# Local attention: values folded with the output weights before the weighing, fixed key blocks, four accumulating banks

## The chip, the cores and the metric

The kernel runs on one core of one Trainium2 chip. The metric is the device time of one execution in microseconds (us). The profile is one execution taken by the hardware profiler. PE is TensorE's matmuls, PEld its weight loads, DVE is VectorE, ACT ScalarE, POOL GpSimd, SP the queue that issues DMAs. Line numbers such as L1101 are those of the kernel before.

## What is computed

x is 2 x 1024 tokens of 128 features, all in fp32. A grouped latent attention and a stack of six layers both work on the normalised x, and both are added to it. The heads are 16 of 64, the window is 32, DEPTH is 6. Shortened:

```python
x = L0_attn_x
xn = _layernorm(x, axis=-1)
x = x + latent_attention(xn) + local_stack(xn)
# local_stack, for each layer i:
x = attn_layer(shift_tokens(x), Wqkv[i], q_scale[i], k_scale[i], Wo[i]) + x
x = ffn_layer(shift_tokens(x), ln_g[i], ln_b[i], W1[i], b1[i], W2[i], b2[i]) + x
# shift_tokens: the second half of the features comes from the token before
# attn_layer:
qkv = x @ Wqkv;  q, k, v = jnp.split(qkv, 3, -1)
q = l2norm(q) * qs;  k = l2norm(k) * ksc
q = q * cos * scale + rotate_half(q) * sin * scale
k = k * cos * inv + rotate_half(k) * sin * inv
out = local_attention(q, k, v)      # a block of 32 sees itself and the block before
return out @ Wo
# ffn_layer: xn is the layer norm of x, scaled by g and shifted by bln
hg = xn @ W1 + b1
a, gate = jnp.split(hg, 2, -1)
return a * jax.nn.gelu(gate, approximate=False) @ W2 + b2
```

## The kernel before, in words

The program has a latent stage, up to about 380 us, which the change leaves as it is but for where x lies, and then the local stage: 6 layers x 16 tiles of 128 tokens = 96 tiles. The local stage is a software pipeline. A loop over steps G is written out, and in each step every engine executes a fixed list of functions, each for a tile G minus some lag. The feed-forward part works on chunks of four tiles (`chunk_at(G, lag)`), so its functions run in every fourth step. Engines meet only by semaphores, and each engine works its list strictly in order.

TensorE, per tile: keys and queries are projected (`project`: two halves of 512 columns, three fp32r matmuls each, banks 0 and 1). VectorE multiplies them with rotary tables (`cosine` L934, `sine` L939), ScalarE squares, VectorE sums (L961, L966) and makes the first guess of a reciprocal root (`seeds`, L992 to L1000), ScalarE refines it by logarithm and exponential (L764, L766), and GpSimd multiplies it together and scales (L501, L507, L513). Transposes (`transposes`, L1258, eight 128x128 per call, banks 2 and 3) put keys, queries and probabilities in place. `mask_scores` (L1299) and `scores` (L1310, 64 matmuls of 64x32 with 64 columns) fill banks 4 and 5; VectorE takes maxima (L1005) and subtracts (L1011), ScalarE takes the exponential.

The value path is what the change touches. The weighted sum is taken over the shifted input rows themselves: `input_rows` (L1324) transposes them, ScalarE copies them out (L710), and ten DMAs on SP's queue lay them out by window (`xw`). `weigh` multiplies them with the probabilities in two halves of four 64x128 matmuls of 256 columns; ScalarE copies each half (`copy_lower` L717, `copy_upper` L723). `fold` multiplies the result with the products M of value and output weights of each pair of heads, 16 matmuls of 128x128 in two halves. Those products are made once per layer (`products`). `attended` (L981) adds the sum to x. The residual x lies with features on partitions (`X`, `X1`); `ln_rows` (L1399) transposes it for the layer norm, `normalise_rows` (L1020) applies it, `ln_columns` (L1407) transposes back, `down` is three matmuls per chunk with 512 columns, and `residual` (L1063) adds.

Most matmuls are written by one helper, `mm` at L1101; the tile names and shapes tell them apart. Every fp32 matmul leaves two records in the trace, an fp32r one and a transpose leave one.

## Time and profile before

| | us |
|---|---|
| three runs, median (lowest to highest) | 2047.29 (2044.84 to 2058.95) |
| the profiled execution | 2045.28 |
| its span, first to last instruction | 2043.4 |
| TensorE busy | 1873.4 (92%) |
| VectorE busy | 1656.8 (81%) |
| GpSimd busy | 1331.1 (65%) |
| ScalarE busy | 1264.6 (62%) |

Busy time of TensorE is the union of its records, and a record's duration includes latency; back-to-back records overlap. The distance between two starts is the better price of a piece of work. A wait behind an engine that is not the bound costs nothing.

### The profile page before, as it was taken

The numbers are of one execution on the slowest core, as the hardware profiler recorded it, in microseconds if no ns is written. First come the engines' busy times: TensorE is split into PE (matmuls) and PEld (weight loads), VectorE is DVE, ScalarE is ACT, GpSimd is POOL, SyncE is SP. The second block draws the span as 40 slices with busy tenths as digits, with TensorE's granted clock in tenths as the row PEclk, the third lists the DMA queues.
The fourth block names the chain that finished last, engine by engine and source line by source line (L and its number), as shares of the span: only waits on it lengthen the run. The fifth ranks groups of instructions, "written<-read, shape, count | busy, mean of one in ns | idle before, by whom it ended". The sixth has DMA issues, their size and how long they took to land.

```text
span 2043.4 us, 61163 instructions
## 1 busy us (share of the span) xinstructions
PE 1873.4 (92%) x24364; PEld 1471.0 (72%) x24364; DVE 1656.8 (81%) x2684; ACT 1264.6 (62%) x2082; POOL 1331.1 (65%) x1146
## 2 busy tenths in 40 slices
PE   6888887598999999999999999999999999999996
PEld 4655656477777777777777777777777777777774
DVE  4866866577888898898879998898989889887873
ACT  5766665355666566656655666566666666665653
POOL 3322334477778776787767886777777778776760
PEclk9999998799999999999999999999999999999999
DMA  3000000011001110010111101100111001000001
GB/s 106 2 0 0 0 1 6 22 38 38 22 18 24 39 40 17 22 25 18 39 38 22 24 19 39 37 22 22 25 39 38 20 21 24 18 18 15 19 18 27
DMA packets 76933, 50.06 MB, mean 24 GB/s; under 512 B 17216, under 2 KB 74240, under 8 KB 75008
## 3 DMA queue, kind: packets, MB, share of 16 engines
q1 hardware_dynamic: 76672, 46.39, 9.0%
q8 instruction: 187, 3.06, 0.6%
q14 instruction: 74, 0.61, 0.1%
HBM read 20.11 MB, written 1.05 MB: 10 GB/s over the span
## 4 chain that ended last, share of the span: by engine, by line
PE 62%; DVE 23%; issue 9%; ACT 4%; POOL 1%; DMA 1%; DVEq 0%; SPq 0%; ACTq 0%; POOLq 0%
PE banks L1101 44%; PE banks L1258 9%; DVE arena L939 4%; PE banks L1310 4%; DVE arena L934 3%; DVE small L885 2%; PE banks L1185 2%; DVE small L1005 2%; DVE small L966 2%; PE banks L1299 1%; DVE lnx L1020 1%; DVE small L961 1%; DVE arena L1048 1%; DVE small L997 1%; DVE small L972 1%
## 5 line engine op out<-in xcount | busy, mean ns | idle before, releaser
L1101 PE MATMUL banks<-arena 128*128 128x128 f32 (+3 forms) x4516 | 450.9, 280 | 32.3 <-DMA arena<-in_wqT_dram 10.1
L1101 PEld LDWEIGHTS banks<-arena 128*128 128x128 f32 (+3 forms) x4516 | 426.5, 173 | 69.8 <-issue 19.1
L471 POOL TENSOR_TENSOR arena<-arena 128x1024 f32<-128x1024 f32 x96 | 228.8, 2383 | 110.0 <-DVE arena L939 110.0
L934 DVE TENSOR_TENSOR arena<-banks,tabs 128x1024 f32<-128x1024 f32 x192 | 234.3, 1220 | 62.4 <-PE banks L1258 52.7
L703 ACT ACTIVATE arena<-banks 128x1024 f32<-128x1024 f32 x96 | 98.6, 1027 | 230.9 <-PE banks L1258 230.9
L939 DVE TENSOR_TENSOR arena<-banks,tabs 128x1024 f32<-128x1024 f32 x192 | 232.9, 1213 | 0.2 <-issue 0.2
L466 POOL TENSOR_TENSOR prob<-prob,small 128x1024 f32<-128x1024 f32 x96 | 182.8, 1904 | 74.2 <-DVE small L974 70.3
L476 POOL TENSOR_TENSOR arena<-arena 128x1024 f32<-128x1024 f32 x96 | 228.5, 2380 | 0.0
L1101 PE MATMUL banks<-arena,xwr 64*128 64x256 f32 x1536 | 217.8, 402 | 11.3 <-ACT arena L717 11.3
L1101 PE MATMUL banks<-qkH,xsH 128*128 128x512 f32 x384 | 173.7, 452 | 39.6 <-DVE arena L939 39.6
L1258 PE MATMUL banks<-cst,arena 128*128 128x128 f32 x1536 | 209.5, 280 | 0.1
L513 POOL TENSOR_TENSOR arena<-arena,small 128x1024 f32<-128x1024 f32 x96 | 185.1, 1928 | 14.0 <-POOL arena L476 0.4
L1258 PEld LDWEIGHTS banks<-cst,arena 128*128 128x128 f32 x1536 | 176.7, 143 | 21.0 <-issue 1.7
L1101 PEld LDWEIGHTS banks<-arena,xwr 64*128 64x128 f32 x1536 | 132.2, 186 | 81.7 <-issue 47.8
L501 POOL TENSOR_TENSOR small<-small 128x33 f32<-128x33 f32 x100 | 24.7, 247 | 248.3 <-ACT small L766 248.3
L507 POOL TENSOR_TENSOR arena<-arena,small 128x1024 f32<-128x1024 f32 x96 | 182.8, 1904 | 4.4
L966 DVE TENSOR_REDUCE small<-arena 128x16 f32<-128x1024 f32 x96 | 116.8, 1216 | 83.3 <-ACT arena L679 82.9
L394 POOL TENSOR_TENSOR gqs<-arena,cst 128x128 fp32r<-128x128 f32 x112 | 46.0, 411 | 186.9 <-PE banks L1101 157.2
L668 ACT ACTIVATE arena<-banks 128x1024 f32<-128x1024 f32 x96 | 98.5, 1026 | 95.5 <-PE banks L1101 95.5
L1101 PE MATMUL banks<-qkH,xsL 128*128 128x512 f32 x384 | 155.1, 404 | 0.0
L1101 PE MATMUL banks<-qkL,xsH 128*128 128x512 f32 x384 | 154.2, 402 | 0.0
L1310 PE MATMUL banks<-arena 64*32 64x64 f32 x12288 | 143.8, 226 | 10.4 <-issue 9.1
(135 smaller groups left out, 4217.6 us busy)
## 6 DMA issues: line engine op xcount, KB each, us to landing
xwr<-xwr SPq DMA_DIRECT2D x576, 32.0 KB, 1.9
qkraw<-in_wqk_dram SPq DMA_DIRECT2D x6, 1024.0 KB, 5.2
arena<-in_wvo_dram SPq DMA_DIRECT2D x6, 1024.0 KB, 5.2
xwr<-xwr SPq DMA_DIRECT2D x384, 16.0 KB, 1.8
W<-in_w_dram SPq DMA_DIRECT2D x6, 341.0 KB, 3.1
W<-in_w_dram SPq DMA_DIRECT2D x6, 192.0 KB, 2.7
res<-in_x_dram SPq DMA_DIRECT2D x4, 256.0 KB, 4.2
tabc<-in_tab_dram SPq DMA_DIRECT2D x1, 1024.0 KB, 7.5
```

What stands on the lines that cost most here:

```text
L466: pool.tensor_tensor(p, p, over(den[:, :], 64), ALU.mult).then_inc(s["p_nrm"], 1)
L471: pool.tensor_tensor(kc, kc, ks, ALU.add).then_inc(s["k_add"], 1)
L476: pool.tensor_tensor(qc, qc, qs, ALU.add).then_inc(s["q_add"], 1)
L507: pool.tensor_tensor(heads(kc), heads(kc), over(rs[:, 4, 0:LH], LD), ALU.mult).then_inc(s["k_nrm"], 1)
L513: pool.tensor_tensor(heads(qc), heads(qc), over(rs[:, 4, LH:2 * LH], LD), ALU.mult).then_inc(s["q_nrm"], 1)
L703: act.activation(ptile[:, :, :], two(2).rearrange("p (k t) -> p k t", k=NP), ACT.Copy).then_inc(s["pt_cp"], 1)
L934: dve.tensor_tensor(heads(c), heads(two(0)), table(k % NT, kind), ALU.mult).then_inc(s[done], 1)
L939: dve.tensor_tensor(w.rearrange("p (h z k) -> p h z k", h=LH, z=2), swapped(two(0)), table2(k % NT, kind + 1), ALU.mult).then_inc(s[done], 1)
L966: dve.reduce_sum(rin[:, LH:2 * LH], heads(sqq), AXX).then_inc(s["q_ss"], 1)
L1101: return pe.matmul(o, l, r, start=start, stop=stop)
L1258: ins = pe.transpose(bk(2 + k // 4)[:, P * (k % 4):P * (k % 4 + 1)], src[:, P * k:P * (k + 1)], ident)
L1310: ins = pe.matmul(bk(4 + o)[WIN * w:WIN * (w + 1), 64 * j:64 * (j + 1)], qT[r, j, WIN * w:WIN * (w + 1)], kT[r, j, WIN * w:WIN * w + 64], ...
```

## The change

The products of value and output weights are made per layer as before, but split into two fp32r parts (`MH` by ScalarE, `ML` by VectorE's `folded_lower`), and each tile's shifted input is multiplied with them at once (`values`, even and odd heads, banks 4 and 5). ScalarE copies the results, 64 rows at a time, into a ring of six half tiles, `vw`, with 64 keys of the even head on partitions 0 to 63 and of the odd one on 64 to 127. `weigh` then takes probabilities as the stationary operand and `vw` as the moving one, and accumulates over all heads into four banks; VectorE adds the four into the residual. Key blocks of 32 no longer slide: a key block stays on the partitions where it is (`keys_of`, new masks), so a window of odd number is one matmul over 128 rows, and one of even number is four over 32 rows each. The input rows' transposes, copies and DMAs go. The residual (`Xt`) has tokens on partitions: `down` is turned round into 12 matmuls of 128 columns with its bias in a row of ones, `ln_rows` is one matmul with a shift matrix and one for the first row, and `layer_columns` transposes x once per chunk for the next layer. The seeds move from VectorE to GpSimd, with `rin` double. `normalise_rows` is a scalar_tensor_tensor in place of a tensor_scalar. The order of the functions is new on all engines, with larger lags, and STEPS grows from 96 + 11 to 96 + 12. The core of the diff:

```diff
+PV_BANKS, V_BANK, XT_BANK, DN_BANK, LN_BANK = (6, 7, 2, 3), 4, 7, 7, 7
...
+        def keys_of(w):
+            return (slice(0, 5, 4), slice(0, 2, 1), slice(2, 0, -1), slice(2, 4, 1))[w]
...
-                sp.wait_ge(s["xT_cp"], k + 1)
-                if k > 1:
-                    sp.wait_ge(s["z_mm"], 2 * k - 2)
-                now, was = xr[:, k % 2, :], xr[:, (k + 1) % 2, :]
-                for o in range(2):
-                    c0 = 64 * o
-                    sp.dma_start(xw[c0:c0 + WIN, k % 2, 0, :], was[96:P, :]).then_inc(xd_in, 16)
-                    sp.dma_start(xw[c0 + WIN:c0 + 64, k % 2, 0, :], now[0:WIN, :]).then_inc(xd_in, 16)
-                    for w in range(1, NW):
-                        sp.dma_start(xw[c0:c0 + 64, k % 2, w, :], now[WIN * (w - 1):WIN * (w + 1), :]).then_inc(xd_in, 16)
                 if n == 2 and l + 1 < DEPTH:
                     sp.wait_ge(s["wk_L"], l + 1)
                     sp.wait_ge(s["wq_L"], l + 1)
                     load_qk(l + 1)
-                if n == 5 and l + 1 < DEPTH:
+                if n == 3 and l + 1 < DEPTH:
                     sp.wait_ge(s["M_mm"], 2 * l + 2)
                     load_wvo(l + 1)
+                if n == 13 and l + 1 < DEPTH:
+                    sp.wait_ge(s["w1_L"], l + 1)
+                    sp.wait_ge(s["b1_mm"], l + 1)
+                    load_w1(l + 1)
...
+            def seeds(k):
+                if is_tile(k) or is_tile(k - 4):
+                    if is_tile(k):
+                        pool.wait_ge(s["k_ss"], k + 1)
+                        pool.wait_ge(s["q_ss"], k + 1)
+                    after(pool, "ln_eps", k - 3)
+                    after(pool, "rk", k)
+                    pool.tensor_scalar(rs[:, 0, :], rin[:, k % 2, :], 1e-24, None, ALU.max).then_inc(s["r_cl"], 1)
+                    pool.wait_ge(s["r_cl"], k + 1)
+                    pool.tensor_scalar(rs[:, 1, :].bitcast(mybir.dt.int32), rs[:, 0, :].bitcast(mybir.dt.int32), -0.5,
+                                       float(0x5F3759DF), ALU.mult, ALU.add).then_inc(s["r_y0"], 1)
+                    pool.wait_ge(s["r_y0"], k + 1)
+                    pool.tensor_tensor(rs[:, 2, :], rs[:, 1, :], rs[:, 1, :], ALU.mult).then_inc(s["r_q"], 1)
+                    after(pool, "y_ln", k)
+                    pool.wait_ge(s["r_q"], k + 1)
+                    pool.tensor_tensor(rs[:, 3, :], rs[:, 2, :], rs[:, 0, :], ALU.mult).then_inc(s["r_r"], 1)
...
-            def copy_lower(k):
...
-            def copy_upper(k):
...
+            def copy_values(k, o):
+                act.wait_ge(s[f"v_mm{o}"], k + 1)
+                after(act, "o_mm", k - 1)
+                for g in range(2):
+                    act.activation(vw[64 * o:64 * o + 64, (2 * k + g) % RV, :], two(V_BANK)[64 * g:64 * g + 64, :], ACT.Copy)\
+                       .then_inc(s[f"v_cp{o}"], 1)
...
+                    act.activation(lns[:, k % 2, 64:D], bk(LN_BANK)[:, 0:64], ACT.Copy).then_inc(s["ln_cp"], 1)
+                    act.activation(lns[:, k % 2, 0:64], Xt[:, k % TILES, 0:64], ACT.Copy).then_inc(s["ln_cp"], 1)
+            def copy_layer(c):
+                if c is not None and c < (DEPTH - 1) * NC:
+                    act.wait_ge(s["xT_mm"], c + 1)
+                    act.wait_ge(s["xs_L"], 2 * (c + NC))
+                    act.activation(xf[:, :], bk(XT_BANK), ACT.Copy).then_inc(s["xT_cp"], 1)
...
             def attended(k):
                 if is_tile(k):
-                    b, i = tile_at(k)
                     dve.wait_ge(s["o_mm"], k + 1)
-                    after(dve, "x_new", (k - TILES) // 4 + 1)
-                    dve.tensor_tensor(X1[:, b, 1 + P * i:1 + P * (i + 1)], bk(M_BANK)[:, 0:P],
-                                      X[:, b, XO + P * i:XO + P * (i + 1)], ALU.add).then_inc(s["x1"], 1)
-            def seeds(k):
...
+                    x1 = Xt[:, k % TILES, :]
+                    for n, bank in enumerate(PV_BANKS):
+                        after(dve, "x1", NW * k + n)
+                        dve.tensor_tensor(x1, bk(bank)[:, 0:D], x1, ALU.add).then_inc(s["x1"], 1)
...
-                    dve.tensor_scalar(lnx[:, :], lns[:, k % 2, :], ag[:, k % 2, 0:1], rs[:, 4, 32:33], ALU.subtract, ALU.mult)\
-                       .then_inc(s["ln_x"], 1)
+                    dve.scalar_tensor_tensor(lnx[:, :], lns[:, k % 2, :], ag[:, k % 2, 0:1],
+                                             rs[:, 4, 32:33].to_broadcast([P, D]), ALU.subtract, ALU.mult).then_inc(s["ln_x"], 1)
...
+            def folded_lower(l, r):
+                dve.wait_ge(s["M_H"], 2 * l + r + 1)
+                dve.tensor_tensor(halves(ML, r), two(2).rearrange("p (o n) -> p o n", o=2), halves(MH, r), ALU.subtract)                   .then_inc(s["M_L"], 1)
...
+            def values(k, o):
+                b, i = tile_at(k)
+                xH, xL = xsH[:, b, P * i:P * (i + 1)], xsL[:, b, P * i:P * (i + 1)]
+                pe.wait_ge(s["xs_L"], 2 * (k // 4) + 2)
+                pe.wait_ge(s["M_L"], 2 * (k // TILES) + 2)
+                claim(V_BANK, V_BANK + 1)
+                for h in range(2):
+                    c0 = HD * o + 512 * h
+                    mm(bk(V_BANK + h), xH, MH[:, c0:c0 + 512], True, False)
+                    mm(bk(V_BANK + h), xH, ML[:, c0:c0 + 512], False, False)
+                    ins = mm(bk(V_BANK + h), xL, MH[:, c0:c0 + 512], False, True)
+                ins.then_inc(s[f"v_mm{o}"], 1)
...
+            def weigh(k):
                 if is_tile(k):
                     pe.wait_ge(s["pt_cp"], k + 1)
-                    pe.wait_ge(xd_in, XD * (k + 1))
-                    weigh(k, 0)
-            def weigh_upper(k):
-                if is_tile(k):
-                    weigh(k, 1)
-            def fold(r):
-                for q in range(4):
-                    for o in range(2):
-                        ins = mm(bk(M_BANK)[:, 0:P], M[:, r, o, q, :], zT[:, o, :, 4 * r + q, :],
-                                 (r, q, o) == (0, 0, 0), (r, q, o) == (1, 3, 1))
-                return ins
+                    pe.wait_ge(s["v_cp0"], 2 * k + 2)
+                    pe.wait_ge(s["v_cp1"], 2 * k + 2)
+                    pe.wait_ge(s["vw_0"], 1)
+                    claim(*PV_BANKS)
+                    def part(n, w, j, r, at, first, last):
+                        return pe.matmul(bk(PV_BANKS[n])[WIN * w:WIN * (w + 1), 0:D], ptile[r, j, WIN * w:WIN * (w + 1)],
+                                         vw[r, at % RV, D * j:D * (j + 1)], start=first, stop=last, skip_group_check=True)
+                    for j in range(NP):
+                        for w in range(0, NW, 2):
+                            g = 2 * k + w // 2
+                            part(j % NW, w + 1, j, slice(0, P), g, j < NW, j >= NP - NW)
+                            for n in range(NW):
+                                ins = part(n, w, j, slice(WIN * n, WIN * (n + 1)), g - n % 2, j == 0, j == NP - 1)
+                    ins.then_inc(s["o_mm"], 1)
+                    for bank in PV_BANKS:
+                        freed[bank] = ("x1", NW * k + NW)
...
+                    n = k % TILES
+                    pe.wait_ge(s["x1"], NW * k + NW)
+                    claim(LN_BANK)
+                    ins = mm(bk(LN_BANK)[:, 0:64], next_row, Xt[:, n, 64:D])
+                    if n % NT:
+                        ins = pe.matmul(bk(LN_BANK)[0:32, 0:64], first_row, Xt[96:P, n - 1, 64:D], start=False, stop=True,
+                                        skip_group_check=True)
...
-                    for j in range(3):
-                        m = FJ[j][1]
-                        ins = mm(bk(DN_BANK), W2[0:m, c // NC % 2, j, :], gl[j][0:m, :], j == 0, j == 2)
+                    for t in range(4):
+                        for j in range(3):
+                            m = FJ[j][1] + (j == 2)
+                            ins = mm(bk(DN_BANK)[:, P * t:P * (t + 1)], gl[j][0:m, P * t:P * (t + 1)], W2[0:m, c // NC % 2, j, :], j == 0, j == 2)
...
+                transpose_keys(G - 2)
+                values_even(G - 2)
+                weigh(G - 4)
+                project_queries(G - 1)
+                ln_rows(G - 4)
+                transpose_queries(G - 2)
+                values_odd(G - 2)
+                down(chunk_at(G, 12))
+                up_value(chunk_at(G, 11), 0)
+                up_value(chunk_at(G, 10), 1)
+                next_products_lower(G - 2)
+                up_value(chunk_at(G, 10), 2)
+                up_gate(chunk_at(G, 9), 0)
+                up_gate(chunk_at(G, 9), 1)
+                transpose_probs(G - 3)
+                next_shifts(chunk_at(G, 11))
+                mask_scores(G - 2)
+                layer_columns(chunk_at(G, 14))
+                scores(G - 2)
+                up_gate(chunk_at(G, 9), 2)
+                next_products_upper(G - 2)
                 project_keys(G)
-                input_rows(G - 2)
-                transpose_keys(G - 1)
-                weigh_lower(G - 3)
-                up_gate(chunk_at(G, 9), 0)
-                up_value(chunk_at(G, 10), 0)
-                next_products_lower(G - 4)
-                up_gate(chunk_at(G, 9), 1)
-                up_value(chunk_at(G, 11), 2)
-                up_value(chunk_at(G, 10), 1)
-                down(chunk_at(G, 12))
-                weigh_upper(G - 3)
-                next_shifts(chunk_at(G, 12))
-                next_products_upper(G - 4)
-                project_queries(G)
-                transpose_queries(G - 1)
-                up_gate(chunk_at(G, 9), 2)
-                fold_lower(G - 3)
                 ln_columns(G - 5)
-                mask_scores(G - 1)
-                fold_upper(G - 3)
-                scores(G - 1)
-                transpose_probs(G - 2)
-                ln_rows(G - 3)
-                last_rows(chunk_at(G, 13))
```

## Rows read from the trace of the kernel before

**Rows 1.** The page: busy us (share) and instructions, and granted clock in 40 slices

```profile
PE 1873.4 (92%) x24364; PEld 1471.0 (72%) x24364; DVE 1656.8 (81%) x2684; ACT 1264.6 (62%) x2082; POOL 1331.1 (65%) x1146
...
PEclk9999998799999999999999999999999999999999
```

**Rows 2.** The page: chain that ended last, by line

```profile
PE banks L1101 44%; PE banks L1258 9%; DVE arena L939 4%; PE banks L1310 4%; DVE arena L934 3%; DVE small L885 2%; PE banks L1185 2%; DVE small L1005 2%; DVE small L966 2%; PE banks L1299 1%; DVE lnx L1020 1%; DVE small L961 1%; DVE arena L1048 1%; DVE small L997 1%; DVE small L972 1%
```

**Rows 3.** Busy by stage, 500 to 1900 us; columns as its first row

```profile
core 0: us, PE busy (x) PEld busy (x) DVE busy (x) ACT busy (x) POOL busy (x), PEclk, DMA share, GB/s
...
500.00:1900.00 1400.00, 1353.42 (x18863) 1072.23 (x18861) 1227.81 (x1665) 894.83 (x1327) 1046.61 (x773) 1.00 0.11 26
```

**Rows 4.** Waits, 500 to 1900 us: who, for whom, us in total, times, longest

```profile
POOL small L501 <- ACT small L766: 196.3, 83, 4.9
...
PE banks L1101 <- DVE arena L939: 23.6, 34, 0.9
...
PEld banks L1101 <- ACT arena L717: 14.8, 20, 0.8
```

**Rows 5.** TensorE's timeline of a tile: start, us, line, out<-in, tile rows*columns, shape

```profile
812.87 0.28 PE L1324 MATMUL banks<-cst,X 64*128 64x64 f32 x2
813.07 1.09 PE L1258 MATMUL banks<-cst,arena 128*128 128x128 f32 x8
814.10 1.13 PE L1101 MATMUL banks<-arena,xwr 64*128 64x256 f32 x8
815.16 0.47 PE L1101 MATMUL banks<-xnH,W1H 128*85 128x512 f32 x1
...
817.74 0.47 PE L1101 MATMUL banks<-qkH,xsH 128*128 128x512 f32 x1 [0.25 <-DVE arena L939]
...
819.21 1.03 PE L1258 MATMUL banks<-cst,arena 128*128 128x128 f32 x8
820.08 1.95 PE L1101 MATMUL banks<-arena 128*128 128x128 f32 x16
821.87 0.27 PE L1407 MATMUL banks<-cst,lnx 128*128 128x128 f32 x1
...
822.41 1.95 PE L1101 MATMUL banks<-arena 128*128 128x128 f32 x16
824.29 1.48 PE L1310 MATMUL banks<-arena 64*32 64x64 f32 x128
825.70 1.09 PE L1258 MATMUL banks<-cst,prob 128*128 128x128 f32 x8
...
830.82 2.84 PE L1101 MATMUL banks<-arena,W 128*128 128x512 f32 x6
833.59 1.14 PE L1101 MATMUL banks<-arena,xwr 64*128 64x256 f32 x8
```

**Rows 6.** TensorE's timeline in the latent stage

```profile
214.87 1.96 PE L1101 MATMUL banks<-arena 128*32 128x128 f32 x64 [0.55 <-ACT arena L624]
216.75 0.33 PE L1185 MATMUL banks<-cst,arena 128*128 128x128 f32 x1
```

**Rows 7.** VectorE by line and form, 500 to 1900 us: busy, mean ns | idle before

```profile
L1020 DVE TENSOR_SCALAR lnx<-lns,small 128x128 f32<-128x128 f32 x82 | 107.9, 1316 | 0.0
...
L966 DVE TENSOR_REDUCE small<-arena 128x16 f32<-128x1024 f32 x83 | 100.9, 1216 | 71.3 <-ACT arena L679 70.9
...
L1000 DVE TENSOR_TENSOR small<-small 128x33 f32<-128x33 f32 x83 | 47.6, 573 | 8.6
...
L981 DVE TENSOR_TENSOR X<-banks,X 128x128 f32<-128x128 f32 x83 | 23.8, 287 | 16.9 <-PE banks L1101 16.7
...
L992 DVE TENSOR_SCALAR small<-small 128x33 f32<-128x33 f32 x83 | 20.0, 241 | 7.7
```

**Rows 8.** ScalarE by line and form, same window

```profile
L717 ACT ACTIVATE arena<-banks 128x1024 f32<-128x1024 f32 x82 | 84.2, 1027 | 3.7
```

**Rows 9.** GpSimd by line and form, same window

```profile
L501 POOL TENSOR_TENSOR small<-small 128x33 f32<-128x33 f32 x83 | 20.5, 246 | 196.3 <-ACT small L766 196.3
```

354 lines of the change are left out of this document (149 added, 205 removed).

## Prediction

> **What bounds the kernel now.** I read the page's busy shares first, then the granted clock, the table by stage, the waits, and the timeline of one tile. TensorE is busy 92% of the span, VectorE 81%, and the granted clock is at 0.9 or more in all slices but two [rows 1]. The chain that ended last is mostly TensorE's lines (44% L1101) with VectorE's rotary and reduction lines in it [rows 2]. Between 500 and 1900 us, a stretch of pure local attention, TensorE is busy 1353.4 of 1400 us at clock 1.00 [rows 3], and 83 tiles pass (the count of L966 in the same window) [rows 7]. So a tile takes 1400 / 83 = 16.87 us, in which TensorE works 16.31 us, VectorE 14.79, ScalarE 10.78 and GpSimd 12.61 (busy over 83), and TensorE stands still 0.56 us. The waits that stop TensorE are short: VectorE's L939 (23.6 us over 83 tiles) and ScalarE's zT copy L717 (14.8 us for the weight loads) [rows 4]. The 196 us of GpSimd behind ScalarE's L766 [rows 4] cost nothing by themselves; they are the other engines' slack. The number that matters is therefore TensorE's work per tile, 96 tiles long; each 0.1 us of it is 9.6 us of the time.
>
> A record's own length is latency. What it costs the queue is the distance from its start to the next start, so all prices below are such distances.
>
> **What is removed from TensorE, per tile.** The first weigh half runs from 814.10 to 815.16, 1.06 us, and there are two: 2.12. The first fold half, 820.08 to 821.87, is 1.79; the second, 822.41 to 824.29, is 1.88: together 3.67. The input rows, 812.87 to 813.07, are 0.20 [rows 5]. Sum 5.99 us.
>
> **What is added.** (1) values: twice the six 128x512 matmuls of a projection. One projection is 817.74 to 819.21, 1.47 us [rows 5]; I take 1.5 each, 3.0. (2) weigh, new. For each of 8 j and two w it issues one matmul of K=128, M=32, N=128 into column group w+1, and four of K=32, M=32 into column group w, each on its own 32 rows and its own bank. No row shows the K=32 form. The nearest with M=32 is the latent stage's outputs: 64 records (two per fp32 matmul) of 128x32 with N=128 take 214.87 to 216.75, 1.88 us less the leaving [rows 6]. That is 16 rounds of four records of about 0.11 us, which is also what one full 128x128 record costs (8 transposes, 819.21 to 820.08, 0.87 us) [rows 5]. So four column groups run at once. The program puts the two records of one matmul next to each other, and still four different ones run at once; the engine does not hold a free sub-array back for a busy one. Rows run at once too: a weigh half is 8 records of N=256 in 1.06 us, where one after another they would take 8 x 0.22 = 1.76. If all this carries over, the new weigh has 8 x 2 x 4 column turns, four at a time: 16 rounds x 0.11 = 1.76 us. (3) Changing the shape costs something. After the input rows the 8 transposes take 1.03 us (813.07 to 814.10) where they take 0.87 elsewhere; the weigh half takes 1.06 where 4 x 0.22 = 0.88 is work [rows 5]. So a change costs 0.16 to 0.18 us. The new weigh has one on the way in and one out: 0.35, so 2.1 us in all, the lower bound of this term. (4) ln_rows becomes two full records of N=64 (weight-load bound, 0.22) and, for seven tiles of eight, two of 32x32 with two shape changes: 0.6 against 0.2, so +0.4. (5) layer_columns, four transposes per four tiles, 0.11 and a little: +0.15. (6) down goes from 6 records of N=512, 830.82 to 833.59, 2.77 us [rows 5], to 24 records at 0.11, 2.64: nothing. Projections, transposes, mask, scores and the up products stay.
>
> Sum: 3.0 + 2.1 + 0.4 + 0.15 - 5.99 = -0.34 us per tile.
>
> **VectorE.** The four seed instructions go to GpSimd: their means run from 241 ns (L992) to 573 ns (L1000), four of them 1.42 us [rows 7]. normalise_rows takes 1316 ns for 128 columns in the before kernel, against 287 for the 128-column add L981 [rows 7]; the length is a wait, because the work is the same size. It turns into a scalar_tensor_tensor. Its mean is bounded by 0.3 (no wait) and 1.3 (unchanged); I take 0.6, by L1000, which also reads two SBUF operands beside GpSimd: -0.7. The Trainium skill, "SBUF — State Buffer", section "Who interferes with whom", says that a tensor_scalar in a two-port mode and an operation with two SBUF inputs both contend with GpSimd's reads; by it the wait does not vanish, and the trace agrees as far as L1000's 573 ns go. Attended becomes four adds for one: +0.9. Folded_lower is 2.4 us a layer: +0.15. VectorE: 14.8 - 1.42 - 0.7 + 0.9 + 0.15 = 13.7. **ScalarE** loses two 1.03 us copies [rows 8] and a small one and gets four copies of 64x1024, which I price as 128x1024 since the free size is the same, one more small row copy and the layer copy: 10.78 + 2.06 + 0.15 = 13.0. **GpSimd** gets four instructions of 33 columns at 0.25 us (its own L501) [rows 9]: 13.6. All three lie under TensorE's 15.97. The 10 row DMAs per tile go; no wait of TensorE ends on them, so they are worth nothing.
>
> **The stalls.** The 0.56 us holds 0.28 for L939 and about 0.2 for L717, which no longer exists. Against that, ScalarE's step with the three gelu has about 17 us of work once 13.0 is its mean, above TensorE's 16, and each layer boundary now puts a VectorE subtraction between products and values. New waits come in too. weigh claims four banks and waits for the values' copies; behind it in TensorE's queue stand the query projection and ln_rows, and through them VectorE's cosine and ScalarE's square. roots on ScalarE now waits for GpSimd's seeds, with gelu and the probabilities' copy behind it. The larger lags (scores at G-2, weigh at G-4) give each of them about a step of room. On SP's queue the row DMAs leave and two weight loads change steps; load_wvo(0) no longer waits for the latent stage, where one 2 to 3 us wait goes. STEPS grows by one, but the last down stays at step 104, so fill and end are priced at nothing; one more filled step would be at most 16 us, which the range holds. I leave 0.45 us of stall: 15.97 + 0.45 = 16.42 us a tile, 0.45 less. 96 x 0.45 = 43 us. The latent stage does not change. The profiled execution has a span of 2043.4 and a time of 2045.3, 2.0 under the median of the three runs (2047.3). 2045.3 - 43 = 2002; on the median's footing 2004. I predict 2003.
>
> **The rivals.**
> *A, the tiles overlap (the forecast).* Chance 0.48, times from 1950 (stalls gone, ScalarE hidden: 0.9 us x 96 = 87, and a few more from the fill) to 2025.
> *B, shapes don't overlap.* The new weigh changes between 128x32 and 32x32 32 times per tile. If the array must run empty at each change, no column works beside another: each of the 16 groups is 2 x 0.11 for the full matmul and 2 x 0.11 for the four small ones, 7.0 us, and 32 changes at 0.17 are 5.4: 12.4 us for 2.1. That is +10.3 - 0.34, or +10 us x 96: about 3000. Without the cost of changes but with the order kept it is 7.4, +4.9 us a tile, about 2515. For it: each shape change in the trace costs. Against it: all those changes are between forms that need the same sub-arrays, and here columns 1 and 3 always hold the full form and 0 and 2 always the small one. No row shows two forms on disjoint columns. It decides early: three of the 32 changes paid (0.5 us) eat the gain. Chance 0.20. The Trainium skill, "TensorEngine Tiling (Array Packing)", section "Tiling Modes", says that changing the mode, not just the tile, drains TensorE; by that rule this case is the one that comes, and the trace's 0.17 us per change agrees with the rule for forms that share sub-arrays.
> *C, half overlap or ScalarE.* If the pairs w=0 and w=2 don't overlap, weigh is 32 rounds, 3.5 us: +1.76 - 0.34, +136 us, 2180. If ScalarE keeps 4.5 of its present 6.1 us of waiting, its 13.0 make 17.5 us a tile: +60, 2105. That ScalarE has such long waits now speaks for it, the wider lags (scores G-2, weigh G-4) against. Chance 0.15, 2066 to 2200.
> *D, the gain is eaten.* The scores' 128 records of N=64, eight sub-arrays at once, would be 16 rounds of 0.055 and a change, 1.05 us; they take 1.41 (824.29 to 825.70) [rows 5], so small tiles don't always reach their rounds. A weigh with the same 0.4 and a little more, 2.6, makes 16.5 of work and with 0.45 of stall 16.9 us: 2050. Chance 0.17, 2025 to 2066.
>
> **How the numbers follow.** About 1% is what a measurement of this kernel can tell from no change, 20 us. A gives faster, nearly all of 0.48; D gives same, 0.17; B and C give slower, 0.35. The forecast is A's 2003. The range leaves out B alone, whose 2500 to 3000 lies apart: 1950 to 2200 holds A, C and D, 0.80. A's own range is 1950 to 2025.
>
> **What would show it.** In the profile after: a weigh group (160 records, forms 128*32 and 32*32) that spans 2.1 us, up to 2.5; at 7 or 12 rival B holds. values at 1.5 us a half. TensorE busy near 15.9 us a tile with stall under 0.5. VectorE at about 13.7 with L1020's successor near 0.6; ScalarE near 13. A tile period near 16.4. The prediction is wrong if weigh is over 2.5 us, if TensorE's stall grows beyond 0.8 us a tile, or if ScalarE's copies end the waits of TensorE.

## The result, and the profile after

The changed kernel takes 2880.27 us, the median of four runs (2875.52 to 2882.36). The kernel before, run beside it, takes 2047.76 (2044.84 to 2058.95, four runs). The ratio is 1.405, with a 95% interval of 1.399 to 1.410. The profiled execution took 2880.3 us with a span of 2878.5. The forecast was 2003 with a range up to 2200; what came is rival B, which said about 3000.

The page of the kernel after, first its busy time and granted clock, then the chain that ended last by engine and line, then the two costliest groups of instructions:

```profile
PE 2663.5 (93%) x36740; PEld 1690.2 (59%) x36740; DVE 1652.5 (57%) x2586; ACT 1448.5 (50%) x2294; POOL 1426.7 (50%) x1543
...
PEclk9999889999999999999999999999999999999997
...
PE 62%; DVE 20%; issue 8%; ACT 7%; POOL 2%; DVEq 0%; DMA 0%; ACTq 0%; SPq 0%; POOLq 0%
PE banks L1361 36%; PE banks L1114 19%; PE banks L1270 3%; DVE prob L1010 3%; DVE small L1004 3%; DVE lnx L1019 3%; DVE small L900 2%; DVE arena L954 2%; DVE small L989 1%; DVE small L983 1%; PE banks L1197 1%; ACT arena L788 1%; DVE Xt L999 1%; ACT arena L723 1%; PE banks L1322 1%
...
L1361 PE MATMUL banks<-arena 32*32 32x128 f32 (+1 forms) x15360 | 1067.5, 282 | 24.1 <-ACT arena L704 22.0
L723 ACT ACTIVATE arena<-banks 64x1024 f32<-64x1024 f32 x384 | 391.9, 1021 | 1015.1 <-PE banks L1361 998.0
```

Against [rows 1] the clock is the same (0.985 over the execution, 0.982 before), so this is not a slower TensorE but more of its time: VectorE's share falls from 81% to 57% although its busy microseconds hardly change. Against [rows 2] one line now heads the chain, L1361, the new weigh, with 36%. Its 15,360 records cost 1067.5 us, 11.1 us for each of 96 tiles. ScalarE's 1015 us of idle time ahead of L723 is the same 1000 us seen from the other side: L723 copies the values into the ring `vw`, and it may overwrite a place there only once the weigh that read it is done.

The table by stage, 700 to 2600 us (local attention alone, after the latent stage), answers [rows 3]. Columns: span of the stretch, then busy (records) of PE, PEld, DVE, ACT, POOL, then clock, DMA share, GB/s:

```profile
700.00:2600.00 1900.00, 1821.24 (x26456) 1131.73 (x26456) 1090.60 (x1430) 947.49 (x1358) 1014.04 (x991) 1.00 0.03 8
```

L1010 and L1019 run 74 times in it, so a tile takes 1900 / 74 = 25.7 us where it took 16.87. TensorE works 24.6 of that, VectorE 14.7, ScalarE 12.8, GpSimd 13.7, and TensorE stands still 1.1 us. The longer period explains the time: 8.8 us x 96 = 845 against 833 measured.

The waits of the same stretch (engine, line, what it waited for: us in all, times, longest) answer [rows 4]:

```profile
ACT arena L723 <- PE banks L1361: 780.7, 74, 11.5
DVE Xt L999 <- PE banks L1361: 715.3, 74, 10.0
POOL prob L462 <- DVE small L991: 678.3, 75, 10.1
...
PE banks L1114 <- DVE prob L1010: 28.5, 53, 1.0
```

All three other engines wait once a tile, some 10 us each: two of them for weigh, GpSimd for a VectorE instruction that stands behind the one that waits for weigh. TensorE itself waits for little. TensorE's timeline of one tile, to be laid beside [rows 5], has the same columns (start, length, line, out<-in, tile rows*columns, shape):

```profile
1405.08 0.39 PE L1114 MATMUL banks<-MH,xsL 128*128 128x512 f32 x1
1405.40 11.06 PE L1361 MATMUL banks<-arena 128*32 128x128 f32 x160
1416.38 0.49 PE L1114 MATMUL banks<-qkH,xsH 128*128 128x512 f32 x1
...
1417.94 0.41 PE L1114 MATMUL banks<-Xt,cst 128*128 128x64 f32 x2
1418.27 0.29 PE L1401 MATMUL banks<-Xt,cst 32*32 32x64 f32 x2
1418.50 1.09 PE L1270 MATMUL banks<-cst,arena 128*128 128x128 f32 x8
```

The weigh's 160 records run from 1405.40 to 1416.38 without a stop: 10.98 us, not 2.1. The steps of the forecast beside it hold: ln_rows takes 1417.94 to 1418.50, 0.56 us for 0.6. One of weigh's sixteen groups in the single records of the trace: the full matmul's two records start at 0 and 0.13 us, the first records of the four small matmuls together at 0.34, their second ones at 0.47, and the next group's full one at 0.69. That is four turns of 0.11 (0.44) and two changes of form of 0.125, and 16 x 0.687 = 10.98. Within a form, different rows run at once; across the two forms nothing does.

### The profile page after: what moved, and what is told of

Same layout as the page of the kernel before. It is cut to its first block, busy times and chain, and to the rows that moved or that the text cites. A ratio compares the mean times of both kernels' runs of the same rounds, so it can differ in the third digit from the quotient of the medians.

```text
span 2878.5 us, 85877 instructions
## 1 busy us (share of the span) xinstructions
PE 2663.5 (93%) x36740; PEld 1690.2 (59%) x36740; DVE 1652.5 (57%) x2586; ACT 1448.5 (50%) x2294; POOL 1426.7 (50%) x1543
## 4 chain that ended last, share of the span: by engine, by line
PE 62%; DVE 20%; issue 8%; ACT 7%; POOL 2%; DVEq 0%; DMA 0%; ACTq 0%; SPq 0%; POOLq 0%
PE banks L1361 36%; PE banks L1114 19%; PE banks L1270 3%; DVE prob L1010 3%; DVE small L1004 3%; DVE lnx L1019 3%; DVE small L900 2%; DVE arena L954 2%; DVE small L989 1%; DVE small L983 1%; PE banks L1197 1%; ACT arena L788 1%; DVE Xt L999 1%; ACT arena L723 1%; PE banks L1322 1%
## 5 line engine op out<-in xcount | busy, mean ns | idle before, releaser
L1361 PE MATMUL banks<-arena 32*32 32x128 f32 (+1 forms) x15360 | 1067.5, 282 | 24.1 <-ACT arena L704 22.0
L723 ACT ACTIVATE arena<-banks 64x1024 f32<-64x1024 f32 x384 | 391.9, 1021 | 1015.1 <-PE banks L1361 998.0
L1361 PEld LDWEIGHTS banks<-arena 32*32 32x32 f32 (+1 forms) x15360 | 446.4, 104 | 655.6 <-issue 654.6
L999 DVE TENSOR_TENSOR Xt<-banks,Xt 128x128 f32<-128x128 f32 x384 | 111.9, 292 | 947.4 <-PE banks L1361 937.6
L1114 PE MATMUL banks<-MH,xsH 128*128 128x512 f32 x384 | 167.2, 435 | 38.6 <-DVE prob L1010 38.6
L682 ACT ACTIVATE arena<-banks 128x1024 f32<-128x1024 f32 x96 | 98.6, 1028 | 177.3 <-PE banks L1114 177.0
L1019 DVE SCALAR_TENSOR_TENSOR lnx<-lns,small 128x128 f32<-128x128 f32 x96 | 153.0, 1594 | 27.6 <-POOL small L515 26.9
L1322 PEld LDWEIGHTS banks<-arena 64*32 64x32 f32 x12288 | 127.6, 105 | 41.4 <-issue 41.4
L1114 PE MATMUL banks<-MH,xsL 128*128 128x512 f32 x384 | 151.6, 395 | 0.0
L1114 PE MATMUL banks<-ML,xsH 128*128 128x512 f32 x384 | 151.4, 394 | 0.0
```

Source lines behind the costliest of these rows:

```text
L723: act.activation(vw[64 * o:64 * o + 64, (2 * k + g) % RV, :], two(V_BANK)[64 * g:64 * g + 64, :], ACT.Copy)\
L1019: dve.scalar_tensor_tensor(lnx[:, :], lns[:, k % 2, :], ag[:, k % 2, 0:1], rs[:, 4, 32:33].to_broadcast([P, D]), ALU.subtract, ALU.mult).t ...
L1114: return pe.matmul(o, l, r, start=start, stop=stop)
L1361: return pe.matmul(bk(PV_BANKS[n])[WIN * w:WIN * (w + 1), 0:D], ptile[r, j, WIN * w:WIN * (w + 1)], vw[r, at % RV, D * j:D * (j + 1)], sta ...
```

## The experiments

Every kernel ran beside the kernel before on the same chip. The three questions in order: does the change of form cause it; could another order or cutting rescue the design; and what would the work have brought if weigh had cost what was forecast.

**f1_grouped: all full matmuls first, then all small ones.** The same 80 matmuls with one change inside weigh for 31.

```diff
                     for j in range(NP):
                         for w in range(0, NW, 2):
-                            g = 2 * k + w // 2
-                            part(j % NW, w + 1, j, slice(0, P), g, j < NW, j >= NP - NW)
+                            part(j % NW, w + 1, j, slice(0, P), 2 * k + w // 2, j < NW, j >= NP - NW)
+                    for j in range(NP):
+                        for w in range(0, NW, 2):
                             for n in range(NW):
-                                ins = part(n, w, j, slice(WIN * n, WIN * (n + 1)), g - n % 2, j == 0, j == NP - 1)
+                                ins = part(n, w, j, slice(WIN * n, WIN * (n + 1)), 2 * k + w // 2 - n % 2, j == 0, j == NP - 1)
```

> The new kernel with the same 80 matmuls of a weigh, but all 16 of 128x32 first and all 64 of 32x32 after them: 2 changes of form a tile where there were 32 inside. In the profile of the new kernel one group (a full matmul and four small ones) takes 0.687 us, which is four record turns of 0.11 and 0.25 us over, 0.125 a change. Theory 1 (each change of form empties the whole array): two columns at a time, 16 rounds and 16 rounds of 0.11 and two changes, 3.8 us for 10.98, so 2880 - 96 x 7.2 = 2190 us. Rival 2 (the 32x32 form is itself slow, or the full and small forms stand in each other's way at the banks, whatever the order): the small ones alone keep over 5 us, 2350 us or more. Rival 3 (the queue only keeps its order and the change is free): 3.5 us, 2160 us, and no gap of 0.1 us at the change.

Measured: 2211.41 us (two runs), ratio 1.080 (1.073 to 1.088). From the timeline of TensorE:

```profile
1416.71 4.24 PE L1361 MATMUL banks<-arena 128*32 128x128 f32 x160 [1.10 <-ACT arena L704]
1420.88 0.51 PE L1114 MATMUL banks<-qkH,xsH 128*128 128x512 f32 x1
```

This tile's weigh runs 4.17 us; the median over the tiles is 3.83. The work is the same and the order alone gives back 7.15 us of 10.98. Two parts of it can be told apart. The 32 full records now pair columns 1 and 3 and the 128 small ones pair 0 and 2, so the turns fall from 64 to 32 (3.5 us less), and 30 changes go, at (7.15 - 3.5) / 30 = 0.12 us each. By the single records of the trace the 32 full ones take 1.87 us and the 128 small ones 1.96 (medians, each with the change behind it), so neither form is slow by itself. Every matmul writes the same bank as in the kernel after. Which writes to one bank come together does change with the order, and no run tests that alone.

**f3_by_j: for each j both full matmuls, then the eight small ones.** The turns are as few as in f1, but the forms change 14 times more.

```diff
                     for j in range(NP):
                         for w in range(0, NW, 2):
-                            g = 2 * k + w // 2
-                            part(j % NW, w + 1, j, slice(0, P), g, j < NW, j >= NP - NW)
+                            part(j % NW, w + 1, j, slice(0, P), 2 * k + w // 2, j < NW, j >= NP - NW)
+                        for w in range(0, NW, 2):
```

> The new kernel with both 128x32 matmuls of a j first and its eight of 32x32 after them: 16 changes a tile, half of the 32. Theory 1: per j 0.22 + 0.22 + 2 x 0.125 = 0.69 us, 5.5 us a tile, 2880 - 96 x 5.5 = 2355 us. If the cost were that of overlap alone, with free changes, 3.5 us and 2160 us.

Measured: 2383.43 us (one run, against 2047.9 for before).

```profile
1410.14 5.83 PE L1361 MATMUL banks<-arena 128*32 128x128 f32 x160
1415.90 0.50 PE L1114 MATMUL banks<-qkH,xsH 128*128 128x512 f32 x1
```

1410.14 to 1415.90 is 5.76 us, 1.93 more than f1's 3.83. Over 14 changes that is 0.14 us each, with the same turns in both kernels. So the price is that of a change, and it is paid although the two forms never hold the same column. The three orders give one model, turns x 0.11 plus changes x 0.125 to 0.14: 3.5 + 0.3 (f1), 3.5 + 2.2 (f3), 7.0 + 4.0 (after).

**f2_one_form: every full matmul cut into four of K=32.** No change of form is left inside weigh, and all 16 sub-arrays have work; the price is 256 records for 160.

```diff
-                        for w in range(0, NW, 2):
+                        for w in range(NW):
                             g = 2 * k + w // 2
-                            part(j % NW, w + 1, j, slice(0, P), g, j < NW, j >= NP - NW)
                             for n in range(NW):
-                                ins = part(n, w, j, slice(WIN * n, WIN * (n + 1)), g - n % 2, j == 0, j == NP - 1)
+                                at = g if w % 2 else g - n % 2
+                                ins = part(n, w, j, slice(WIN * n, WIN * (n + 1)), at, j == 0, j == NP - 1)
```

> The new kernel with each 128x32 matmul of the odd windows cut into four of 32x32, so that weigh has one form alone: 128 matmuls, 256 records, on all 16 sub-arrays. More instructions than now (256 records for 160). Theory 1: 16 rounds of 0.11 and two changes, 2.1 us, TensorE's work back near 16 us a tile, so 2880 - 96 x 8.9 = 2025 us, between 1990 and 2060; the rest of the recorded sum is then tested too, since that is the 2.1 us it assumed. Rival 2 (32x32 slow, or issue of 256 records at 11 ns and more): 2.9 to 4 us, 2100 to 2200 us.

Measured: 2417.09 us (four runs), ratio 1.179 (1.172 to 1.186). Theory 1 was wrong. Rival 2 has the work of weigh (2.9 to 4 us) but not the time (2100 to 2200), and for a reason that neither theory held. TensorE's timeline of one tile:

```profile
1411.79 2.32 PE L1361 MATMUL banks<-arena 32*32 32x128 f32 x160
1415.55 1.48 PE L1361 MATMUL banks<-arena 32*32 32x128 f32 x96 [1.44 <-issue]
1416.95 0.50 PE L1114 MATMUL banks<-qkH,xsH 128*128 128x512 f32 x1
```

Two things are seen. First, the records between pauses take 2.32 and 1.40 us; over all tiles it is 3.65 us for 256 records, 14.3 ns each. That is eight at a time by turns of 0.11 us, as f1 had it with half as many sub-arrays, not sixteen. In the 88 weighs that ran wholly at TensorE's upper clock level (2.4 GHz) this work is 3.54 us, 13.8 ns a record. Second, TensorE stops for 1.44 us in the middle, and the reason given is "issue": nothing that the profile shows held it. The mean over the tiles is 2.3 us of such pauses.

The position of the pauses names their cause. Counting TensorE's instructions from the start, 139 of its 201 stalls of over 0.9 us (after 400 us) start at one and the same position modulo 256, that is, a whole multiple of 256 instructions apart. The page's row of the queue that brings the instructions, first in before, then in f2, has 187 and 356 packets:

```profile
q8 instruction: 187, 3.06, 0.6%
```

```profile
q8 instruction: 356, 5.83, 1.0%
```

5.83 MB / 356 is 16,384 bytes each. The 169 packets more belong to some 43,400 more TensorE instructions in f2's trace, 257 for each packet. In the tile above a block of 256 was entered at 1412.10, the next packet started at 1412.88 and took 1.2 us, and the next block's first instruction ran at 1415.55, 1.47 us after the packet had landed. At 138 of the 140 block edges with a stall of over 0.9 us this last step takes 1.2 to 1.6 us, so the stall ends with the packet and not with another engine. The median from entering a block to the next packet is 1.14 us, and the quickest blocks take 3.0 to 3.3 us (5th percentile in f2, g1, g2 and g4). A long run of matmuls that each take 14 ns uses its block up in 1.8 us (128 records, each with its weight load), faster than the next arrives. In before only 9 of 57 such stalls stand at the position.

**g1_half_cols: f2 with 64 moving columns for 128.** Half of each attended output is left out.

```diff
-                        return pe.matmul(bk(PV_BANKS[n])[WIN * w:WIN * (w + 1), 0:D], ptile[r, j, WIN * w:WIN * (w + 1)],
-                                         vw[r, at % RV, D * j:D * (j + 1)], start=first, stop=last, skip_group_check=True)
+                        return pe.matmul(bk(PV_BANKS[n])[WIN * w:WIN * (w + 1), 0:D // 2], ptile[r, j, WIN * w:WIN * (w + 1)],
+                                         vw[r, at % RV, D * j:D * j + D // 2], start=first, stop=last, skip_group_check=True)
```

> f2_one_form with 64 of the 128 moving columns in each 32x32 matmul of weigh (so half of each head's output is left out of the sum; the count of matmuls and of weight loads is unchanged). f2 took 3.65 us a tile for its 256 records once its pause is taken off, 14.3 ns a record, where 16 sub-arrays at once would give 1.75. If the columns set it (some sub-arrays wait for others), 64 columns take about half, 1.9 us. If weight loads or the issue of records set it, 3.3 us or more stay. In both cases the pause of 1.7 to 1.8 us that every weigh of f2 has stays or grows if it comes from the supply of instructions, since these are as many.

Measured: 2485.58 us (one run). Weigh is 2.85 us without its pauses, 11.1 ns a record, and the pauses are 2.98.

```profile
1407.42 1.86 PE L1361 MATMUL banks<-arena 32*32 32x64 f32 x170 [0.55 <-ACT arena L704]
1411.35 1.07 PE L1361 MATMUL banks<-arena 32*32 32x64 f32 x86 [2.07 <-issue]
```

Neither expectation for the work holds: half the columns save 22% of it, not half and not nothing. A record with 64 columns costs 11 ns, as it does in the scores of [rows 5] (128 records in 1.41 us), and the columns still count at 128. Which part of the engine sets either is open. The pauses stay, as expected: 155 of 212 stalls stand at the block position. That the total got slower with less work is not explained by weigh, which with its pauses takes 5.8 us a tile for 6.0 in f2. The clock differs: the granted clock of this execution is 0.918 against 0.964, with TensorE at its lower level (1.2 GHz) for 410 us of the span against 174. The granted clock in 40 slices, in f2 and in g1:

```profile
PEclk9999988999999999999999999999999999999996
```

```profile
PEclk9999988898999989889898989998989999988996
```

An estimate from these numbers is that 236 us more at half the clock cost up to 118 us. In the weighs that ran wholly at the upper level (46 in g1, 88 in f2) the work takes 2.70 us for 3.54 and the pauses 2.32 for 2.26, so longer pauses are not shown either. Why the clock stood lower more often is open.

**g2_rows_outer: f2 with the loop over rows outside that over columns.**

```diff
                     for j in range(NP):
-                        for w in range(NW):
-                            g = 2 * k + w // 2
-                            for n in range(NW):
+                        for n in range(NW):
+                            for w in range(NW):
+                                g = 2 * k + w // 2
```

> f2_one_form with the two inner loops of weigh exchanged: for each j the 32-row groups outside, the column groups inside. Same matmuls. If the queue's order decides how many sub-arrays run at once, the 3.65 us without the pause changes by over 0.5 us either way; if load or issue per record decides, it stays within 0.2.

Measured: 2519.08 us (one run). Weigh without pauses is 3.86 us, 0.21 more than f2, and the pauses are 2.33, as in f2. The mean granted clock of this execution was 0.914, against 0.964 in f2's, so the kernel's time itself is not compared. The 0.21 us are the clock's too: in the 40 weighs wholly at the upper level the work takes 3.54 us, as in f2. The order of the sub-arrays isn't what holds them at eight.

**g4_split: f2's weigh in two halves, one ahead of the query projection and one behind it.** If a block of instructions lasts longer, the next arrives in time.

```diff
-            def weigh(k):
+            def weigh(k, js):
...
-                weigh(G - 4)
+                weigh(G - 4, range(0, NP // 2))
                 project_queries(G - 1)
+                weigh(G - 4, range(NP // 2, NP))
```

> f2_one_form with weigh in two halves of four j, the query projection (1.5 us, 12 instructions) between them. Same instructions in another order, and two changes of form more (+0.25 us a tile, +24 us). In f2 all 138 pauses inside runs of short matmuls stand at distances of whole multiples of 256 instructions in TensorE's stream, which is 16 KB, the size of the instruction queue's packets. Theory S (the supply of instructions by 16 KB block is outrun by short matmuls): the pause of 2.3 us a tile shrinks to under 1, 2417 falls to 2280 to 2340. Theory W (the pause is a wait for another engine or for a bank): it stays, 2420 to 2450.

Measured: 2478.13 us (two runs), ratio 1.213 (1.209 to 1.216), 60 us over f2. The time is more than both theories allow, so it decides nothing by itself. The timeline of one tile:

```profile
1414.98 1.49 PE L1363 MATMUL banks<-arena 32*32 32x128 f32 x97
1418.25 0.51 PE L1363 MATMUL banks<-arena 32*32 32x128 f32 x31 [1.78 <-issue]
...
1420.27 1.44 PE L1363 MATMUL banks<-arena 32*32 32x128 f32 x91
1422.11 0.84 PE L1363 MATMUL banks<-arena 32*32 32x128 f32 x37 [0.40 <-issue]
1424.39 0.42 PE L1114 MATMUL banks<-Xt,cst 128*128 128x64 f32 x2 [1.45 <-DVE Xt L999]
```

Waits of TensorE from 700 to 2200 us, some 70 tiles, first in f2, then in g4:

```profile
PE banks L1361 <- issue: 142.3, 94, 2.6
```

```profile
PE banks L1114 <- DVE Xt L999: 103.1, 70, 2.0
...
PE banks L1363 <- issue: 40.6, 34, 2.8
```

This tile still has pauses, of 1.78 and 0.40 us, but over all tiles they shrank. Each half is 128 records of two instructions each, so it holds 256 instructions and meets one edge of a block, and the two halves meet 192 edges as f2's weighs do. In f2 126 of them carry a pause of over 0.35 us, in g4 56, and the pauses inside weigh fall from 2.3 to 0.76 us a tile. That is theory S, the supply of instructions. Its time didn't come, because the edit laid bare another wait: `ln_rows` needs VectorE's four adds of the same tile's weigh (L999). In f2 the query projection stood between the two, in g4 nothing does, and TensorE waits 1.47 us a tile. The two added changes of form cost about 0.25 us more. What is left of the 60 us is not told apart; the granted clock is 0.953 for 0.964. An order that keeps other work ahead of `ln_rows` as well wasn't tried. Without any pause f2 would still take about 2200 us (2417 less 96 x 2.3, an estimate), more than before.

**k1_small_once: f1 with the small matmuls for the first j alone.** Seven eighths of the weighing of the even windows are left out. Weigh then costs about what was forecast, and the rest of the forecast can be seen.

```diff
-                    for j in range(NP):
+                    for j in range(1):
                         for w in range(0, NW, 2):
                             for n in range(NW):
-                                ins = part(n, w, j, slice(WIN * n, WIN * (n + 1)), 2 * k + w // 2 - n % 2, j == 0, j == NP - 1)
+                                ins = part(n, w, j, slice(WIN * n, WIN * (n + 1)), 2 * k + w // 2 - n % 2, True, True)
```

> f1_grouped with the 32x32 matmuls of weigh for the first pair of heads only: seven eighths of the weighing of the even windows is left out of the output, and everything else of the new kernel stays. weigh then costs 1.75 (128x32, two columns at a time) + 0.22 + three changes of 0.13, 2.3 us, close to the 2.1 that the recorded sum assumed. So the run shows what the rest of that sum was worth. If the other terms hold (TensorE's work 13.5 + 2.3 = 15.8, stall 0.45), 2000 us. If the stalls of f1 (TensorE idle 1.18 us a tile, of which ScalarE's copy of the probabilities) come from elsewhere than weigh, 16.9 us a tile and 2050 to 2070 us.

Measured: 2046.47 us (eight runs), ratio 1.001 (0.999 to 1.003): no change. The table by stage, two waits of the same stretch, and the timeline of weigh with the even values ahead of it:

```profile
700.00:1900.00 1200.00, 1118.42 (x17316) 878.68 (x17316) 1035.57 (x1358) 904.38 (x1294) 960.66 (x940) 1.00 0.03 10
```

```profile
PE banks L1114 <- DVE prob L1010: 30.6, 50, 1.4
...
PE banks L1361 <- ACT arena L704: 18.3, 21, 1.1
```

```profile
1301.00 0.47 PE L1114 MATMUL banks<-MH,xsH 128*128 128x512 f32 x1 [0.49 <-DVE prob L1010]
...
1302.56 2.32 PE L1361 MATMUL banks<-arena 128*32 128x128 f32 x48
1304.80 0.50 PE L1114 MATMUL banks<-qkH,xsH 128*128 128x512 f32 x1
```

Some 70.5 tiles pass, 17.0 us each. Weigh takes 2.25 us and TensorE works 1118.4 / 70.5 = 15.9 us, as the forecast's sum had it (15.97). The stall is 1.16 us where 0.45 was taken. It has two main parts: the even values claim banks that the score subtraction L1010 on VectorE frees (0.43 us a tile), and weigh waits for ScalarE's copy of the probabilities L704 (0.26). Both stand in the kernel after too, with 28.5 and 17.6 us over 74 tiles. So the gain of 0.4 us of work would have gone into new waits even with the weigh that was forecast.

**f4_before_rows: the kernel before, with the key transposes ahead of the input rows.** It applies the finding to before: input rows and weigh_lower both have 64-row tiles, the transposes between them have 128. Putting the two together saves two changes a tile.

```diff
                 project_keys(G)
-                input_rows(G - 2)
                 transpose_keys(G - 1)
+                input_rows(G - 2)
                 weigh_lower(G - 3)
```

> The kernel before with one line of TensorE's order moved: input_rows (64x128) stands behind transpose_keys (128x128), directly ahead of weigh_lower (64x128), so a tile has two changes of form fewer. Theory 1 (a change costs 0.12 to 0.17 us wherever it is, and TensorE sets the time): 0.25 to 0.35 us a tile, 24 to 33 us, 2015 to 2025 us. Rival (the seams are waits for other engines or ScalarE's copies come later and stop the DMA path): 2040 to 2060 us.

Measured: 2033.66 us (ten runs), ratio 0.9952 (0.9919 to 0.9985): 14 us under before by the medians, 10 by the ratio, and half or less of what was expected.

```profile
1013.07 1.03 PE L1258 MATMUL banks<-cst,arena 128*128 128x128 f32 x8
1014.04 0.28 PE L1324 MATMUL banks<-cst,X 64*128 64x64 f32 x2
1014.15 1.08 PE L1101 MATMUL banks<-arena,xwr 64*128 64x256 f32 x8
1015.16 0.47 PE L1101 MATMUL banks<-xnH,W1H 128*85 128x512 f32 x1
```

```profile
PEld banks L1101 <- ACT arena L717: 33.4, 63, 0.9
```

The input rows cost 0.11 us (1014.04 to 1014.15) for 0.20 in [rows 5], the three pieces together 2.09 us (1013.07 to 1015.16) for 2.29 (812.87 to 815.16), and the work over 500 to 1900 us falls from 1353.42 to 1344.56 us. Part is given back: TensorE comes sooner to the fold that needs ScalarE's zT copy L717, and the wait of its weight loads for it rises from 14.8 us [rows 4] to 33.4.

**h2_norm_act, h3_seeds_pool, h4_norm_late: VectorE's relief, on f4.** The forecast had VectorE 1.1 us a tile shorter. These ask what relief is worth, and why L1020 lasts 1316 ns [rows 7]. h2 leaves VectorE one column and gives the normalising to ScalarE:

```diff
-                    dve.tensor_scalar(lnx[:, :], lns[:, k % 2, :], ag[:, k % 2, 0:1], rs[:, 4, 32:33], ALU.subtract, ALU.mult)\
-                       .then_inc(s["ln_x"], 1)
+                    dve.scalar_tensor_tensor(small[:, 501:502], ag[:, k % 2, 0:1], -1.0, rs[:, 4, 32:33], ALU.mult, ALU.mult)\
+                       .then_inc(s["ln_nb"], 1)
...
+                    act.activation(lnx[:, :], lns[:, k % 2, :], ACT.Identity, bias=small[:, 501:502], scale=rs[:, 4, 32:33])\
+                       .then_inc(s["ln_x"], 1)
```

> f4_before_rows (2034 us) with normalise_rows moved: VectorE only makes the product of mean and reciprocal root for each token (one column), ScalarE scales and shifts the 128 columns. Takes about 1.1 us a tile off VectorE (14.8 to 13.7, what the recorded sum expected of the change) and puts 0.3 on ScalarE. If VectorE's load is part of TensorE's 0.5 us of stall, up to 0.3 us a tile goes, 2005 to 2025 us; if not, 2030 to 2040.

Measured: 2044.55 us (ten runs) against 2043.44, ratio 1.000 (0.998 to 1.002). That is about 0.5% over f4's ratio and outside both expected ranges; the relief cost time, and TensorE's wait for ScalarE's zT copy L717 rose from 6.8 us in f4 to 17.6 (500 to 1900 us). The row of VectorE's remaining instruction, by line and form:

```profile
L1028 DVE SCALAR_TENSOR_TENSOR small<-small 128x1 f32<-128x1 f32 x82 | 98.4, 1200 | 0.0
```

One column takes 1200 ns where 128 took 1316: the length isn't work. In before, 93 of the 96 records of L1020 began while a GpSimd instruction was under way and end 81 to 130 ns after its end, 87 of them 81 to 87 ns after; the three that met none took 336 to 340 ns. The Trainium skill, "SBUF — State Buffer", section "Who interferes with whom", lets an operation with two SBUF inputs, as in h2, and a tensor_scalar in a two-port mode contend with GpSimd. The trace agrees that both wait; in which mode the tensor_scalar L1020 ran it does not show.

h4 moves the instruction to where GpSimd is idle, behind the seeds:

```diff
-                normalise_rows(G - 5)
...
                 seeds(G)
+                normalise_rows(G - 5)
```

with ScalarE's copy_columns and TensorE's ln_columns moved behind it.

> f4_before_rows (2034 us) with normalise_rows behind the seeds on VectorE, at the moment when GpSimd has nothing to do, and ln_columns and its copy later by as much. In the profile of before, 93 of 96 of these instructions end 81 to 87 ns after the end of the GpSimd instruction that was under way at their start, and the three that met none take 0.34 us. If the length is that wait, the mean falls from 1.3 to 0.34-0.5 us and VectorE's busy time from 14.8 to about 13.9 a tile. If VectorE then stops TensorE less (25 us of waits for L939 over 83 tiles), 2010 to 2030 us; if the freed time goes into other waits, as in h3, 2030 to 2050.

Measured: 2038.58 us (eleven runs) against 2045.62, ratio 0.9964 (0.9946 to 0.9983). Its line, and one wait of TensorE:

```profile
L1020 DVE TENSOR_SCALAR lnx<-lns,small 128x128 f32<-128x128 f32 x83 | 28.4, 343 | 0.0
```

```profile
PE banks L1407 <- DVE lnx L1020: 36.0, 25, 1.8
```

The instruction falls from 1.3 to 0.34 us, as long as the three in before that met no GpSimd instruction. VectorE is busy 13.9 us a tile for 14.8, and the kernel is no faster than f4, whose interval overlaps. TensorE now waits 0.43 us a tile for the later result instead.

h3 gives the four seed instructions to GpSimd, as the change did:

```diff
+                seeds(G)
                 refine(G)
...
                 sum_queries(G)
-                seeds(G)
```

> f4_before_rows (2034 us) with one part of the change alone: the four seed instructions on GpSimd in place of VectorE, ahead of refine, rin single with waits. VectorE 14.8 to 13.4 us a tile, GpSimd 12.6 to 13.6. If VectorE's queue makes the 0.28 us that TensorE waits for L939, it gains up to 0.25 us a tile: 2010 to 2025 us. If not, 2030 to 2040; if GpSimd's chain (seeds, roots, refine, scale) gets later, 2040 to 2070.

Measured: 2049.05 us (seven runs) against 2044.71, ratio 1.003 (1.000 to 1.006), so about 0.8% over f4's ratio. VectorE is down to 13.6 us a tile, and two waits are new:

```profile
ACT small L783 <- POOL small L511: 133.9, 57, 4.7
...
PE banks L1261 <- POOL arena L525: 37.2, 24, 2.1
```

GpSimd's own work, now behind the seeds, comes later; the key transposes L1261 wait for its scaled keys. The same move is part of the change. In the kernel after no wait of TensorE for GpSimd is over 0.2 us; weigh gives every engine 10 us of slack.

## Why the prediction was wrong

**What held.** The bound was read rightly: TensorE's work per tile sets the time, and 8.3 us more of it and 0.5 us more stall a tile made 833 us. The terms beside weigh were right or near: values 1.5 us a half, ln_rows 0.56 for 0.6, the work without weigh 13.5 for 13.87, ScalarE 12.8 for 13.0, GpSimd 13.7 for 13.6. That the row DMAs were worth nothing is consistent with this and was not tested by itself.

**The step that failed** is the one that priced weigh, "the engine does not hold a free sub-array back for a busy one". It was taken from [rows 6], where four column groups run at once, and from the 64-row weigh halves in [rows 5], where two row groups do. Both rows show tiles of one form. The forecast carried them over to two forms, on the ground that they lie on disjoint columns, and said itself that no row shows that. Its premise that the two records of one matmul stand next to each other in the queue was read from the program; the trace doesn't name a record's matmul. The runs show the limit: a change of form empties the array wherever the tiles lie. f1 and f3 do the same matmuls with 1 and 15 changes inside weigh and differ by 1.93 us. The term was 2.1 us and measured 10.98: 7.0 of turns that no longer lie beside one another, and 4.0 of changes.

Rival B had this to the term: 7.0 us of turns came as 7.0, and its 32 changes at 0.17 came at 0.125 to 0.14, so it said 12.4 us and about 3000 where 10.98 and 2880 came. The error lay in its chance, 0.20. What spoke against it was an argument (disjoint columns), what spoke for it was every change of form in the trace and the Trainium skill, "TensorEngine Tiling (Array Packing)", section "Tiling Modes". The runs agree with that section: the mode decides, not the tile. The trace's 0.16 to 0.18 was near enough to see that three changes would eat the gain.

**The second error was the stall.** Taken as 0.45 us a tile, it is 1.1 in the kernel after, 1.18 in f1 and 1.16 in k1. The forecast named weigh's claim of four banks and the wider lags, and let them cancel. k1 shows that they don't: the even values wait for the banks that L1010 frees, and weigh waits for L704. By k1, with weigh at 2.25 the kernel would have come out at 2046, not 2003, which is rival D's result by way of the stall and not of weigh. So no single correction of the weigh term would have made the forecast right.

**VectorE** came to 14.7 us a tile for 13.7. Most of it is one line, L1020's successor, taken as 0.6 us:

```profile
L1019 DVE SCALAR_TENSOR_TENSOR lnx<-lns,small 128x128 f32<-128x128 f32 x74 | 119.6, 1617 | 15.0 <-POOL small L515 14.3
```

It takes 1.6. In [rows 7] its forerunner had 1316, and the forecast recognised a wait in that but priced it by L1000, of whose 100 records in before only 25 begin while a GpSimd instruction is under way. What the wait waits for is the end of a GpSimd instruction of some 1.9 to 2.4 us. In the kernel after 92 of 96 end 144 to 151 ns after one does; 49 of them began while it was under way, the other 43 began 42 to 44 ns ahead of it. That it cost the kernel nothing is argued from VectorE's 10 us of waiting a tile, and by h2 to h4 VectorE's relief gains nothing either: on f4, about 1 us less work of VectorE a tile (h3, h4) never made the kernel faster.

**Could the design win?** Not by any of the ways tried. The best order, f1, leaves 13.5 + 3.83 = 17.3 us of work where before has 16.3. Cutting all to one form meets the eight-at-a-time limit and the supply of instructions. By k1 even a weigh near the forecast's 2.1 us would only draw level. The fastest kernel of all is f4, before with two lines exchanged; its interval and h4's overlap.

## What to carry to other kernels

Count the changes of tile form along TensorE's queue and price each at the 0.12 to 0.18 us that this kernel shows, whether or not the forms share columns, and take overlap only between tiles of one form; then put work of one form together, which gave 0.5% for the exchange of two calls. When a step's price rests on a case that no row shows, and the trace's nearest rows all carry a penalty, the penalty is the likely case, not the tail. A saving of a few tenths of a microsecond of work per step is not a saving of time until the engine's new waits have been followed one by one: g4 shortened the pauses as meant and lost it again to a wait that its new order laid bare.

## What the runs showed of the hardware that was not expected

- A change between 128x32 and 32x32 tiles costs 0.125 to 0.14 us on disjoint columns too (after, f1, f3), and nothing of the two forms overlaps.
- 32x32 tiles in fp32 with N=128 run at 14.3 ns a record (13.8 at the upper clock level), as eight at a time would by turns of 0.11 us, no matter whether 8 (f1) or 16 (f2, g2) sub-arrays have work. With N=64 it is 11.1 ns (g1; 10.5 at the upper level). Why is open.
- TensorE's instructions arrive in packets of 16,384 bytes, one for 256 instructions by the positions of the stalls. Short matmuls use a block up in 1.8 us or less, while the quickest blocks take 3.0 to 3.3 us. TensorE then stands still at the edge of the block, 0.4 to 2.1 us at a time in the tiles shown, 2.3 to 3.0 us a tile on average in f2 and g1 and 0.76 where long matmuls stand between two halves (g4). 139 of 201 stalls stand at the position in f2, 155 of 212 in g1, 9 of 57 in before. The profile calls this "issue".
- A small VectorE operation can last as long as a GpSimd instruction: 1200 ns for one column (h2), 343 ns for 128 columns once GpSimd is idle (h4).
